# Regrouping the weighted sums and key sums of a fused attention and recurrence kernel

## The reference

```python
x = x + attn(layernorm(x))          # x: (16, 1024, 256)
x = x + ffn(layernorm(x))

def attn(x):                        # 16 query/key heads of 16 channels, 8 value heads of 32
    q, k, v = x @ Wq.T, x @ Wk.T, x @ Wv.T
    q, k = rope(q) * scaling, rope(k)        # rotation with a decay that depends on the position
    probs = softmax(q k^T)                   # (16 heads, 1024, 1024)
    diff = probs[even heads] - lam * probs[odd heads]
    a = diff @ v                             # per value head
    return (a * rsqrt(mean(a * a) + 1e-5) * KEEP) @ Wo.T

def ffn(x):                         # a recurrence over the 16 sequences
    for xt in x:
        f = sigmoid(xt @ wf.T + c @ uf.T + bf); i = sigmoid(xt @ wi.T + c @ ui.T + bi)
        c = f * c + i * tanh(xt @ wc.T + c @ uc.T + bc)
    return tanh(x @ wo.T + c @ uo.T + bo)    # every sequence, with the last c
```

## Time and profile before

| | |
|---|---|
| median of 3 runs | 5024.14 us (5023.08 to 5025.57) |
| profiled execution, its time | 5025.16 us |
| its span, first to last instruction | 5023.4 us |
| mean granted TensorE clock | 0.988 |
| PE / PEld / DVE | 97% / 35% / 78% of the span busy |
| ACT / POOL | 57% / 58% |
| one iteration, first key tile to first key tile | 298.3 us |

### The profile page before, as it was taken

One profiled execution on the slowest core, in us unless ns is written; L12 is line 12 of the kernel. 1 busy time (PEld: TensorE's weight loads), 2 busy tenths in 40 slices (PEclk: granted clock), 3 DMA queues, 4 the chain that ended last, 5 costly groups with the idle time before them and its releaser, 6 DMA issues.

```text
span 5023.4 us, 67256 instructions
## 1 busy us (share of the span) xinstructions
PE 4887.4 (97%) x24784; PEld 1747.6 (35%) x24784; DVE 3935.0 (78%) x6295; ACT 2883.0 (57%) x5221; POOL 2936.0 (58%) x2134
## 2 busy tenths in 40 slices
PE   7999999999999999999999999999999999999999
PEld 2224242332424333242332424233242433324237
DVE  7878878888887888888887887888888788887526
ACT  1565646656464665646566564665646466564642
POOL 3673827658384774728567382765838477472740
PEclk6999999999999999999999999999999999999999
DMA  5131222213122130322313122221312313022117
GB/s 147 35 65 44 48 70 51 64 36 63 50 51 66 39 72 39 61 55 47 72 34 67 42 47 70 51 63 36 63 49 51 66 39 72 39 53 50 68 52 291
DMA packets 128060, 311.20 MB, mean 62 GB/s; under 512 B 27505, under 2 KB 30706, under 8 KB 113906
## 3 DMA queue, kind: packets, MB, share of 16 engines
q1 hardware_dynamic: 124610, 289.62, 23.9%
q10 hardware_dynamic: 3120, 17.27, 0.9%
HBM read 171.68 MB, written 99.61 MB: 54 GB/s over the span
## 4 chain that ended last, share of the span: by engine, by line
PE 78%; POOL 12%; ACT 5%; issue 3%; DVE 2%; DMA 0%; ACTq 0%; SPq 0%; DVEq 0%; POOLq 0%
PE s_ps L821 15%; PE o_ps L865 15%; PE st L852 14%; PE st L958 13%; POOL pair_sum L502 12%; PE sum_ps L880 7%; PE st L787 4%; PE st L805 4%; ACT probs L610 3%; PE st L1035 2%; DVE neg_max L1157 2%; PE st L936 1%; PE o_ps L774 1%; PE s_ps L1035 1%; PE sum_ps L774 0%
## 5 line engine op out<-in xcount | busy, mean ns | idle before, releaser
L502 POOL TENSOR_TENSOR pair_sum<-probs 128x512 f32<-128x512 f32 x2048 | 2827.8, 1416 | 1176.9 <-ACT probs L610 1176.9
L1157 DVE TENSOR_REDUCE neg_max<-s_ps 128x1 f32<-128x512 f32 x4096 | 2582.1, 682 | 698.8 <-PE s_ps L821 696.5
L610 ACT ACTIVATE probs<-st 128x512 f32<-128x512 f32 x4096 | 2161.6, 604 | 943.8 <-PE st L852 782.5
L821 PE MATMUL s_ps<-k_stack,q_stack 96*128 96x512 bf16 x4096 | 1520.7, 389 | 21.0 <-DVE neg_max L1157 19.4
L852 PE MATMUL st<-q_stack,k_stack 99*128 99x512 bf16 x4096 | 1474.3, 384 | 28.7 <-ACT probs L610 7.5
L865 PE MATMUL o_ps<-probs,values 128*32 128x512 f32 x8192 | 1092.9, 605 | 12.3 <-ACT probs L610 8.5
L852 PEld LDWEIGHTS st<-q_stack,k_stack 99*128 99x128 bf16 x4096 | 368.0, 97 | 1358.1 <-ACT probs L610 908.1
L821 PEld LDWEIGHTS s_ps<-k_stack,q_stack 96*128 96x128 bf16 x4096 | 400.5, 98 | 656.0 <-DVE neg_max L1157 313.5
L880 PE MATMUL sum_ps<-pair_sum,ones 128*32 128x512 f32 x4096 | 535.0, 594 | 26.7 <-POOL pair_sum L502 26.7
L958 PE MATMUL st<-pair_sum,weights 128*128 128x512 f32 x768 | 381.9, 594 | 11.8 <-ACT pair_sum L566 11.8
L560 ACT ACTIVATE probs<-st,gate_bias 128x512 f32<-128x512 f32 x192 | 131.6, 686 | 441.8 <-PE st L958 441.8
(11 more groups left out here) (152 smaller groups left out, 3027.9 us busy)
## 6 DMA issues: line engine op xcount, KB each, us to landing
q_stack<-qk_parts SPq DMA_DIRECT2D x378, 128.0 KB, 4.2
k_stack<-qk_parts SPq DMA_DIRECT2D x378, 128.0 KB, 6.8
swapped<-xa SPq DMA_DIRECT2D x128, 256.0 KB, 2.4
qk_parts<-swapped SPq DMA_DIRECT2D x64, 512.0 KB, 2.8
probs<-in_x SPq DMA_DIRECT2D x16, 1024.0 KB, 9.5
x_rows<-probs SPq DMA_DIRECT2D x16, 1024.0 KB, 3.9
qk_parts<-low_part SPq DMA_DIRECT2D x63, 256.0 KB, 3.0
xa<-in_x SPq DMA_DIRECT2D x15, 1024.0 KB, 5.9
```

The lines of the kernel that those rows point to most:

```text
L502: pool.tensor_tensor(pair_sum[q % 2][:, h, :], probs[a % 4][:, h, :], probs[(a + 1) % 4][:, h, :], ALU.add)\
L610: act.activation(probs[kk % 4][:, h, :], st[n % BANKS][:, :], ACT.Exp).then_inc(exp_done, 1)
L821: pe.matmul(s_ps[i % BANKS][:, :], q_stack[g][0:SROWS, s, t * P:(t + 1) * P], k_stack[g][0:SROWS, s, h * HALF:(h + 1) * HALF], start=True, ...
L1157: dve.tensor_reduce(neg_max2[:, at, i % 2:i % 2 + 1], s_ps[i % BANKS][:, :], AX.X, ALU.max, negate=True).then_inc(max_done, 1)
```

## The change

1. In `attention` on PE the products are grouped otherwise. All four key tiles of a step come in a row, and a function `group` puts products in at three places of each cycle of four steps (16 key tiles): after tile 2 the weighted blocks of the last two steps of the cycle before; after tile 6 key sums 2c - 2 and the weighted block of step 4c; after tile 12 key sums 2c - 1 and the weighted block of step 4c + 1. Steps 30 and 31 and key sums 14 follow the last tile. Before it were four places, one in each step.
2. `ROPE_AT` and `CAST_AT` are spread: the first unit's rotation ends in step 22 (16 before), the second's in step 26 (20). The casts stand in steps 8, 13, 16, 19 and 13, 18, 21, 24.
3. DVE's scaling of finished sums moves one step later (s % 8 == 4, and 5 for `combine`); so do the plans' costs for it.
4. In the gate products, the transposes of the first half go ahead of the third cell part, with its two scores, which stood before them.
5. In the opening, 4 scores follow the last product of qk(1) and 16 go between the value products; the row of scores after them is shorter by these 20.

```diff
--- before.py
+++ after.py
@@ -63,13 +63,13 @@
 BEFORE = EARLY[0]
 NEXT_LN, NEXT_QK = 80, 102
 
-ROPE_AT = ({1: 0, 2: 1, 3: 2, 4: 7, 5: 8, 6: 4, 7: 9, 9: 6, 13: 11, 16: 13},
-           {5: 0, 6: 1, 7: 2, 8: 7, 9: 8, 10: 4, 12: 9, 13: 6, 16: 11, 20: 13})
-CAST_AT = ({4: 3, 7: 5, 11: 10, 14: 12}, {9: 3, 12: 5, 14: 10, 18: 12})
+ROPE_AT = ({1: 0, 3: 1, 5: 2, 7: 7, 9: 8, 10: 4, 14: 9, 15: 6, 17: 11, 22: 13},
+           {5: 0, 7: 1, 9: 2, 13: 7, 15: 8, 16: 4, 18: 9, 22: 6, 23: 11, 26: 13})
+CAST_AT = ({8: 3, 13: 5, 16: 10, 19: 12}, {13: 3, 18: 5, 21: 10, 24: 12})
 SUB_ORDER = (0, 2, 4, 6, 1, 3, 5, 7)
 
 ROPE_WORK = 2.7
-WORK = [[(ROPE_WORK if s in at else 0) + (4 if s > 8 and s % 8 == 3 else 0)
+WORK = [[(ROPE_WORK if s in at else 0) + (4 if s > 8 and s % 8 == 4 else 0)
          for s in range(STEPS)] for at in ROPE_AT]
 WORK[1][0] += 2
 WORK[1][1] += 3
@@ -883,21 +883,32 @@
 
             def attention(u, g, un, plan):
 
+                def group(s, h):
+
+                    c, place = divmod(4 * s + h, 16)
+                    if place == 2 and c > 0:
+                        weighted(u, g, 4 * c - 2)
+                        weighted(u, g, 4 * c - 1)
+                    if place == 6:
+                        if c > 0:
+                            key_sums(u, g, 2 * c - 2)
+                        weighted(u, g, 4 * c)
+                    if place == 12:
+                        if c > 0:
+                            key_sums(u, g, 2 * c - 1)
+                        weighted(u, g, 4 * c + 1)
+
                 pe.wait_ge(shift_in, 48 * (u + 1))
                 for s in range(STEPS):
 
                     todo = list(plan[s])
-                    for h in range(3):
+                    ahead = iter(todo)
+                    for h in range(4):
                         key_tile(u, g, s, h)
-                        for i in todo[h:h + 1]:
+                        for i in itertools.islice(ahead, len(todo) if h == 3 else 1):
                             score(un, 1 - g, i)
-                    if s >= 1:
-                        weighted(u, g, s - 1)
-                    if s >= 4 and s % 2 == 0:
-                        key_sums(u, g, (s - 4) // 2)
-                    key_tile(u, g, s, 3)
-                    for i in todo[3:]:
-                        score(un, 1 - g, i)
+                        group(s, h)
+                weighted(u, g, STEPS - 2)
                 weighted(u, g, STEPS - 1)
                 key_sums(u, g, 14)
 
@@ -969,15 +980,16 @@
                                 score(u + 3, 1, n)
                     return mm
 
+                own = 2 * b + (1 if last else 2)
                 pe.wait_ge(cell_ready, 4 * b + 1)
                 for i in range(BANKS):
+                    if i == BANKS - 1:
+                        transposes(xn2, ln2_out, b, own, halves=(0,))
                     turn(GATE + i, b, ab)
                     gate_part(i, True, True, False)
                     if not last:
                         for n in itertools.islice(late, i):
                             score(u + 2, 0, n)
-                own = 2 * b + (1 if last else 2)
-                transposes(xn2, ln2_out, b, own, halves=(0,))
                 pe.wait_ge(xt_out, 4 * own + 2)
                 for i in range(BANKS):
                     gate_part(i, False, False, True).then_inc(ring_ready, 1)
@@ -1000,12 +1012,13 @@
             transposes(xa, ln1_out, 0, 0)
             pe.wait_ge(xt_out, 4)
             qk(0, 0, 0)
-            qk(1, 0, 0)
+            first = iter(range(SCORES))
+            first_scores = ((0, 0, i) for i in first)
+            qk(1, 0, 0, first_scores, (0,) * 7 + (4,))
             pe.wait_ge(consts_in, N_CONST)
             pe.wait_ge(consts_made, 2)
-            rows_out(VAL[0], W_V, xt, 0, 0)
-            first_scores = ((0, 0, i) for i in range(SCORES))
-            for block in itertools.islice(first_scores, NEXT_QK):
+            rows_out(VAL[0], W_V, xt, 0, 0, beside=(0, 0, first))
+            for block in itertools.islice(first_scores, NEXT_QK - 4 - 4 * TT // 2):
                 score(*block)
             transposes(xa, ln1_out, 1, 1, first_scores)
             pe.wait_ge(xt_out, 8)
@@ -1224,7 +1237,7 @@
             def attention(u, g, un, plan, turned=None):
                 for s in range(STEPS):
                     todo = iter(plan[s])
-                    if s > 8 and s % 8 == 3:
+                    if s > 8 and s % 8 == 4:
                         r = s // 8 - 1
                         turn_sums(u, g, r)
                         for i in itertools.islice(todo, 1):
@@ -1233,7 +1246,7 @@
                         for i in itertools.islice(todo, 1):
                             maximum(un, i)
                         scale(u, g, r)
-                    if s > 8 and s % 8 == 4:
+                    if s > 8 and s % 8 == 5:
                         combine(u, g, s // 8 - 1)
                     for i in todo:
                         maximum(un, i)
```

## The result

The changed kernel takes 5051.2 us (median of 6 runs, 5047.87 to 5053.13) against 5024.85 us (6 runs); the ratio is 1.0045, 95% interval 1.0032 to 1.0057. It is slower by about half a per cent, a small change but clear of the interval. Its profiled execution has a span of 5046.8 us, 23.4 us more than the one before.

The account below looks back on a forecast made before the run. PE, busy 97% of the span, was taken as the bound, with POOL and DVE close behind. +36 us for 15 iterations, about +4 for the last, -7.5 gate products, -6 opening: 5024 + 26 = 5050 us, range 4988 to 5090.

Parts of the forecast that it names:

- Rings: Key tiles and scores waiting for free buffers: first attention 6.35 us against 1.65, second 5.2 against 2.7.
- Casts: ACT's casts behind a run's first tile delay PE: step 13 +1.0 us; second attention's steps 13 and 21 +1.0, +0.8.
- Drains: PE's changes into narrow tiles and back, 0.24 us each: 24 groups for 32 save 1.92 us an attention.
- Pair sums: PE's waits for POOL's additions: spread rotation clears the backlog, -2.5 and -2.3 us, with 0.2 left in each attention.
- The rival that POOL stays behind: Pair sums get less room than 6.8 us, collisions are paid on PE: 5080 us and above, chance 0.13.
- First to last tile: Key tiles of an attention: about 101.0 us in a first and 99.2 in a second (99.5 and 99.4 before).
- Gate products: Moved transposes wait 0.43 us for DVE's norm instead of 0.9 for ACT: -0.47 x 16 = -7.5 us.
- Opening: First maximum starts at about 44.5 us, not 51.49; DVE sets the pace: -6 us, bounds 0 and -7.
- Scaling a step later: DVE's later scaling of finished sums still meets PE's need for them: costs nothing, bound +0.5 us.
- The last iteration: Its second attention has no scores, so each run of six waits 0.96 us: about +4 us.
- a group of the old order hides every cast: Before, each step's last tile began its run, so the group was taken to hide the cast from PE.
- The rival that ACT and DVE keep up: Casts and rotation lag cost less than the 4.2 us an iteration summed: 4982 us at nothing, half-way 5010; chance 0.2.

Follow-up runs that it names:

- e6: Changed kernel, three casts one step earlier, exponentials, maxima and pair sums on half their columns: 4770.47 us, ratio 0.9479 to before.
- e7: Kernel before plus spread rotation and casts, new gate products and opening, with exponentials, maxima and pair sums on half columns: 4830.07 us, ratio 0.9596.
- e4: Changed kernel with the three casts behind step 4c + 1 moved behind step 4c: 5011.55 us, ratio 0.9975 to before.
- e1: Kernel before with only the new grouping and the later scaling (items 1 and 3): 5110.53 us, ratio 1.0172.
- e2: Kernel before with only rotation and casts spread (item 2): 4982.2 us, ratio 0.9917.
- e3: Kernel before with spread rotation and casts, new gate products and opening (items 2, 4 and 5): 4966.49 us, ratio 0.9885.
- e8: e3 with the first attention's casts of steps 8 and 16 moved to 7 and 15, the second's of 24 to 25: 4945.32 us, ratio 0.9826.

## Why the prediction was right

The forecast was 5050 us, measured are 5051.2. The cause and the terms of the attentions hold one by one; that the sum is met to 1 us is luck. The two traces, whose spans differ by 23.4 us, part the time in three: the opening gives -7.4 us (-6 forecast), the first fifteen iterations +31.3 (+29, gate products included), and the last iteration with all that follows it -0.4 (+3.5). The misses cancel in part, and the medians happen to lie 26.4 us apart.

- **Rings.** Subtracting starts in the timeline after, key tiles wait 3.7 us in the first attention and 3.7 in the second without the casts' part (3.7 and 3.5 forecast). Scores wait 3.5 and 2.1 us (2.7 and 1.7 by the ring, with 0.9 and 0.3 for the rotation operation that runs into the next run). e6 and e7 show that it is waiting for the other engines and not TensorE's own work.
- **Casts.** 0.97, 0.98 and 0.67 us (1.0, 1.0, 0.8); e4 took them away and gained 40 us.
- **Drains.** 0.24 us each by the earlier trace rows, 0.23 between the two kernels with idle rings.
- **Pair sums.** Forecast 0.2 us left, found none of note: POOL fell to 1% of the chain. The rival that POOL stays behind didn't come about.
- **First to last tile.** 101.0 and 99.2 us forecast, 100.94 and 99.42 measured.
- **Gate products.** -0.43 us an iteration (-0.47).
- **Opening.** -7.4 us (-6): the first maximum came half a microsecond earlier, and the value products with a score between them didn't fall behind DVE.
- **Scaling a step later.** Costless in the changed kernel as said; e1 shows that it is so only with the spread, which the prediction didn't say.
- **The last iteration.** Up to its last key tile it is 3.6 us longer, about the +4 forecast. What follows, 198.92 us before and 194.87 after, is 4 us shorter, and no term foresaw that. Two pieces of the chain hold most of it, first before, then after:

```profile
4836.12 8.86 PE st L805 x32
...
4910.63 7.11 PE st L1035 x24
```

```profile
4863.91 7.17 PE st L805 x32
...
4935.73 5.42 PE st L1048 x24
```

Each takes 1.69 us less for the same work. Before, the mean granted clock was 0.57 from 4836 to 4840 us and 0.58 from 4911 to 4915; after, it is 1.00 in these places (4863 to 4867, 4938 to 4942). That this follows from the change is not shown. Without it the spans would lie some 27 us apart (an estimate, 23.4 + 2 x 1.69).

One assumption proved wrong without hurting the sum: that a group of the old order hides every cast. It was used for e2 and e3, which missed their forecasts by 32 and 30 us. e8 won 21 us back by moving casts; the remaining 10 us or so are not explained. In the changed kernel the groups next to steps 8 and 16 hold two blocks and do hide copy and cast. The rival that ACT and DVE keep up is half true: e4 shows that the casts' part of it can be had by moving three numbers.

## What to carry to other kernels

Merging small groups to save a drain lengthens the runs between them, and a run can't go faster than its ring of buffers allows, whatever spare time its consumer has elsewhere: compare the saving (here 8 x 0.24 us in an attention) with the time at which the last member of the longer run may start. Write such a rule down, lay it over the order before and see whether it puts each wait of the trace on its place; then lay it over the new order. And when an engine feeds a ring, put its side jobs (casts, copies) where a long group of the other engine follows, and not two in one step. When one part of a change loses and others win, take them apart: the spread, the opening and the gate products alone gained 58 us here, and the grouping lost more than that.

## What the runs showed of the hardware

TensorE's granted clock is at its upper level (2.4 GHz, a PEclk of 1.00) from 164 to 4624 us in the kernel before and from 153 to 4647 us in the changed one, but not in the one with runs of eight. Its windows (length, busy time of PE, PEld, DVE, ACT, POOL, then PEclk) and the timeline of PE in the same place:

```profile
796.00:800.00 4.00, 3.43 (x27) 0.89 (x19) 2.87 (x6) 1.84 (x3) 3.05 (x3) 1.00 0.00 0
800.00:804.00 4.00, 3.17 (x14) 0.82 (x18) 3.53 (x5) 3.61 (x8) 3.18 (x3) 0.79 0.00 0
804.00:808.00 4.00, 3.74 (x24) 0.79 (x16) 1.79 (x3) 0.71 (x2) 3.21 (x2) 0.78 0.00 0
808.00:812.00 4.00, 3.80 (x24) 1.02 (x28) 3.32 (x6) 3.32 (x7) 3.48 (x3) 1.00 0.00 0
```

```profile
800.73 0.88 PE L852 MATMUL st<-q_stack,k_stack 99*128 99x512 bf16 x2 [1.30 <-ACT probs L610]
...
802.62 3.45 PE L865 MATMUL o_ps<-probs,values 128*32 128x512 f32 x16
```

PE waits 1.3 us for an exponential behind copy and cast, the next tiles trickle at ACT's pace, and then the clock is at its lower level (1.2 GHz) for part of two stretches: two weighted blocks take 3.45 us where they take 1.92 in the changed kernel at 851.60. The span's mean clock is 0.981 (0.99 in the changed kernel).

The same trace shows what such a fall costs, since not every attention has one. Two second attentions of this kernel, without and with it:

```profile
579.20:682.60 103.40, 98.00 (x578) 26.48 (x574) 83.10 (x120) 69.31 (x133) 83.38 (x61) 1.00 0.30 62
888.90:993.90 105.00, 99.59 (x578) 26.77 (x574) 83.28 (x120) 69.28 (x133) 83.35 (x61) 0.98 0.28 61
```

From first to last key tile they take 103.37 and 104.95 us. The trace has 24 such falls between 181 and 4683 us; at 1.5 us each, an estimate, they make 36 of the 46 us that the forecast for this kernel missed. e1 has seven in its attentions, the other kernels none. So waits that cluster can cost twice: once themselves, and once in the work behind them. That the waits bring the fall about is read from their order in the trace; no run isolates it.
